# Two more row blocks' halves at the end: the last four tiles of a graph attention kernel as half tiles, in another order

## The reference

```python
XW = jnp.matmul(X, W)
s_col = jnp.matmul(XW, a[0, :f])
s_row = jnp.matmul(XW, a[0, f:])
Z1 = jax.nn.leaky_relu(s_row[:, None] + s_col[None, :], negative_slope=0.01)
den = jnp.exp(Z1)
num = jnp.matmul(A, den)
att = jnp.where(num != 0, den / jnp.where(num != 0, num, 1.0), 0.0)
H = jnp.matmul(A, jnp.matmul(att, XW))
x = _layernorm(x + H, axis=-1)
```

## Time and profile before

| | before |
|---|---|
| median of 3 runs | 309.93 us |
| the profiled execution's own time | 310.36 us |
| its span | 308.6 us |
| TensorE busy | 273.2 us (89%) |
| VectorE busy | 224.5 us (73%) |
| ScalarE busy | 190.1 us (62%) |
| GpSimd busy | 96.0 us (31%) |
| chain that ended last: TensorE's share | 62% |

### The profile page before, as it was taken

The page is one execution under the profiler, slowest core; times in us unless marked ns, Lnnn a source line. Parts: engine busy times, 40 slices in busy tenths (PEclk is TensorE's granted clock), DMA queues, the critical chain, the costliest instruction groups (busy, mean ns, idle before and its releaser), DMA issues.

```text
span 308.6 us, 5025 instructions
## 1 busy us (share of the span) xinstructions
PE 273.2 (89%) x1635; PEld 155.1 (50%) x1635; DVE 224.5 (73%) x363; ACT 190.1 (62%) x245; POOL 96.0 (31%) x95
## 2 busy tenths in 40 slices
PE   8793589788699999999999999999999726999994
PEld 3592337233244544544454445444444202999994
DVE  0778899999789989987985789898797710052275
ACT  2498068698899986959586788879688630000001
POOL 6501277998884644500000000066000063000000
PEclk9855556999999999999999999999999986999998
DMA  5000599707665343510000000001000053201111
GB/s 169 1 2 2 146 322 387 303 3 219 181 201 156 93 139 88 158 63 0 0 2 0 0 2 0 0 29 43 0 2 1 0 170 106 66 2 36 34 36 34
DMA packets 13940, 24.65 MB, mean 80 GB/s; under 512 B 1760, under 2 KB 8288, under 8 KB 13920
## 3 DMA queue, kind: packets, MB, share of 16 engines
q0 software_dynamic: 5632, 18.88, 19.1%
q1 hardware_dynamic: 8288, 5.50, 6.1%
HBM read 21.23 MB, written 3.15 MB: 79 GB/s over the span
## 4 chain that ended last, share of the span: by engine, by line
PE 62%; DVE 7%; ACT 6%; POOL 5%; issue 4%; DMA 4%; ACTq 1%; POOLq 0%; SPq 0%
PE ps L486 25%; PE ps L510 9%; PE ps L546 9%; PE ps L548 5%; PE ps L504 4%; POOL A L314 3%; PE ps L480 2%; PE ps L448 2%; PE ps L446 2%; PE ps L490 2%; DMA A<-adjT,perm 2%; POOL d_b L335 2%; ACT A L607 1%; ACT tmp L626 1%; DMA D<-d_b 1%
## 5 line engine op out<-in xcount | busy, mean ns | idle before, releaser
L486 PE MATMUL ps<-A,D 128*128 x372 | 86.3, 379 | 0.9 <-issue 0.2
L486 PEld LDWEIGHTS ps<-A,D 128*128 x372 | 36.2, 97 | 40.9 <-issue 10.1
L314 POOL DMA_INDIRECT A<-adjT,perm x31 | 45.5, 1468 | 28.3 <-DVE A L206 12.6
L335 POOL DMA_INDIRECT d_b<-crow,ranku x16 | 17.6, 1099 | 109.1 <-DVE crow L1014 71.0
L685 ACT ACTIVATE stage<-ps 128x1024 f32<-128x1024 f32 (+1 forms) x33 | 32.9, 997 | 25.8 <-PE ps L490 25.7
L996 DVE SCALAR_TENSOR_TENSOR stage<-ps,stage 128x1024 f32<-128x1024 f32 (+1 forms) x33 | 39.2, 1188 | 12.8 <-ACT stage L697 12.7
L546 PE MATMUL ps<-D,A 128*128 128x256 f16 x256 | 42.4, 273 | 1.0 <-DMA D<-d_b 1.0
L548 PE MATMUL ps<-D,A 128*128 128x128 f16 x256 | 42.3, 219 | 0.0
L1000 DVE SCALAR_TENSOR_TENSOR stage<-rrow,cfloor,stage 128x1024 f32<-128x1024 f32 (+1 forms) x33 | 41.3, 1252 | 1.3
L206 DVE SCALAR_TENSOR_TENSOR A<-A,ecol 128x1024 f16<-128x1024 f32 x31 | 38.8, 1277 | 1.0 <-ACT A L607 0.4
L687 ACT ACTIVATE stage<-stage,epst 128x1024 f32<-128x1024 f32 (+1 forms) x33 | 37.1, 1123 | 1.1
(11 more groups left out here) (187 smaller groups left out, 367.9 us busy)
## 6 DMA issues: line engine op xcount, KB each, us to landing
tmp<-xT SPq DMA_DIRECT2D x4, 256.0 KB, 4.1
d_xw<-stage SPq DMA_DIRECT2D x1, 1024.0 KB, 5.1
D<-d_b SPq DMA_DIRECT2D x4, 256.0 KB, 3.7
out<-crow SPq DMA_DIRECT2D x3, 256.0 KB, 2.3
A<-adjT,perm POOLq DMA_INDIRECT x31, 5.6
xws<-d_xw,perm POOLq DMA_INDIRECT x16, 3.6
d_b<-crow,ranku POOLq DMA_INDIRECT x16, 2.5
out<-crow SPq DMA_DIRECT2D x1, 128.0 KB, 1.8
```

The costliest lines, as they stand in the source:

```text
L314: nc.gpsimd.indirect_dma_start(out=raw[n], out_offset=None, in_=rows, in_offset=bass.IndirectOffsetOnAxis(ap=perm[:, 0, h, b:b + 1], axis= ...
L486: nc.tensor.matmul(num[bank + c], D[:, d, bass.ds(slot, 1), :], A[:, h, bass.ds(k, 1), a, c * W:(c + 1) * W], start=False, stop=False, ski ...
```

## The change

The last two row blocks of the second half, and no longer the last one alone, are half tiles. `ITEMS` lists all half tiles of the third quarter first and then those of the fourth, so the end of the list goes from (14 full), (15 third), (15 fourth) to (14 third), (15 third), (14 fourth), (15 fourth). `FULL` goes from 31 to 30 and `LAST` from 33 to 34. The second line keeps the set of items that use f16 parts as it is, 16 to 28.

```diff
-HALVED = NB - 1
+HALVED = NB - 2
 LAST = 2 * NB + NB - HALVED
 ITEMS = ([(t // NB, t % NB, 0, 2) for t in range(NB + HALVED)]
          + [(1, J, c, 1) for c in range(2) for J in range(HALVED, NB)])
@@
         def in_halves(t):
 
-            return NB <= t < FULL - 2
+            return NB <= t < FULL - 1
```

## The result

The changed kernel took 316.21 us, the median of 5 runs (315.27 to 316.83), against 310.09 us (309.92 to 310.81) before: 6.1 us slower, a ratio of 1.0183 with a 95% interval of 1.0162 to 1.0203. A second set of runs on another occasion gave 1.0177 (1.0142 to 1.0212). The time lies at the very edge of the predicted range (312.5 to 316.2), and next to the rival in which TensorE's clock falls in the new gap (315.9), not at the forecast of 313.4.

The account below looks back on a forecast made before the run. The prediction took the time as set by when the third quarter's transposes start (245.72 us) plus a fixed remainder. Bank wait, work behind it and end order move them to 249.15: 309.93 + 3.43 = 313.36, said as 313.4 us, range 312.5 to 316.2.

Parts of the forecast that it names:

- The fixed remainder behind the transposes: From the third quarter's transposes through GpSimd's scatters to the end: everything keeps its distance, nothing gives back the 3.43 us.
- First, the bank: Item 30 now takes bank 2, waits for item 29's read, starts at 236.68 not 232.62; TensorE idle 3.9 us.
- Second, the work from there: TensorE from item 30's start at 236.68: half tiles and L510s priced one by one, L510 of item 31 ending at 247.15.
- The second turn of the slot loop: In item 30's two-slot half tile: an estimated 0.10 us added for the branch, bounds 0 and 0.3.
- Third, the order at the end: Third quarter, complete at 247.2, waits behind item 32 on VectorE and TensorE; its transposes start at 249.15.
- The clock: TensorE's granted clock stays 1.00 from 232 to 250 us, through the new gap; this forecast had chance 0.73.
- The clock rival: TensorE's clock falls in the new gap: 2.5 us more, 315.9 us (317.6 with a later return); chance 0.21.
- The sum: Third quarter's transposes at 249.15 against 245.72, 3.43 us later, giving 313.4 us.

Follow-up runs that it names:

- e1: Changed kernel with 16 f16 matmuls that nothing reads put on TensorE ahead of item 30, filling the gap: 315.13 us, ratio 1.0165.
- e8: Second run of the changed kernel with the gap filled by 16 f16 matmuls that nothing reads: 315.43 us.
- e9: Changed kernel with the gap filled by four f32 matmuls in place of 16 f16 ones: 317.99 us in an uneven set, ratio 1.0125.
- e4: Changed kernel with its half tiles' banks swapped and the third quarter's end moved forward: 311.50 us, ratio 1.0031.
- e10: Changed kernel with banks swapped, third quarter's end moved forward, and two unread f32 matmuls between L510 of items 32 and 33: ratio 1.0005, uneven set.
- e5: Changed kernel with the gap filled by 16 unread matmuls and the third quarter's end moved forward: 315.48 us.
- e6: Kernel before, with item 30 (full tile) also waiting for item 29's read and 16 unread matmuls ahead of that wait: 314.59 us, ratio 1.0141.

## Why the prediction was right or wrong

- *The fixed remainder behind the transposes.* Right for the changed kernel: first scatter up 5.33, last 5.31, first L546 5.09. It is not a law, as e1 showed.
- *First, the bank.* Right to the row: 3.90 us of gap, released by item 29's L996; item 30 starts 8.62 us behind item 29, and not 4.46. Swapping the banks takes it away, and adding the wait to the old kernel brings it.
- *Second, the work from there.* 0.4 us too small, as the filled kernel shows at full clock. The second turn of the slot loop costs 0.36 us out of a wait (236.93 to 237.94 is 1.01, three matmuls are 0.65) and not 0.10; item 31 has a stop of 0.17 us behind its L480 (240.44) that I had not counted; item 32, which does not start from a wait, took 1.76 us and not 1.92; and the transposes start 0.96 and not 0.86 us behind L510. 0.26 + 0.19 - 0.16 + 0.10 = 0.39, and 3.43 + 0.39 is the 3.82 of e1 (3.81); e8 and e9 have 3.99 and 4.04.
- *Third, the order at the end.* Right in kind: about 2 us of the 4. To be faster, the prediction wanted the third quarter copied and transposed ahead of item 32, with the wait gone too. That has been tried (e4, e10), and is no gain so far: what is won at the first scatter is spent before the last one or behind it.
- *The clock.* This is the step that failed. I gave the 1.00 through the gap 0.73 and the fall 0.21. It fell in all four profiles. I had one empty stretch to go by, of 2.96 us, in the earlier trace rows, and took the dense work round the new gap for a reason against; a gap of 3.90, longer than one that had brought the fall, was the stronger evidence, and the Trainium skill's rule (TensorE: Matmul & The Clock Gate, "Why this matters for your kernels", against gaps between bursts of matmuls) said so too; here the trace agrees with it: the gap was 3.90 us, and the granted clock fell to 0.50.
- *The clock rival's size.* 2.5 us was too large for its own step: 0.7 to 1.5 us in the profiles, by the way it is measured. Counted from item 30's start, item 31 started 1.3 to 2.0 us later than in e1, not 2.5. In two of four profiles the low level lasted only 3.4 us. In the other two it lasted 6.8, and item 30 still cost 1.0 us more and not 1.5 (236.49 to 239.88, against 236.49 to 238.86 in e1): its six matmuls are one group of 2.74 us, without the stop of the second turn that e1 has. And 0.4 us of it came back behind: after the slow part item 31 ran L480 to L490 in 1.03 us and not 1.36, without the stops for issue.
- *The sum.* The profiled changed kernels are up 4.7 to 5.3 at the first scatter: 4.0 us for wait and order (e9), and 0.7 to 1.3 for the clock. The medians are up 6.1 and 5.3, and the first L546 in the profiles 4.75 to 5.09: 0.2 to 1.4 us are in no profile. That 316.2 lay so near to the rival's 315.9 is partly luck, its parts being 0.6 too small and 1.2 or more too large.

## What to carry to other kernels

When a loop's tail changes its tile size, work out for the first new tile which buffer it takes and who read it last; a rotation that is free of stalls for one parity can wait for its immediate predecessor for the other. An idle stretch of TensorE can be priced twice, once as the wait and once in the matmuls behind it, and one idle stretch in the trace that brought the clock down is to be taken at its word. Filling a gap with matmuls that nothing reads tells the two prices apart, but look at what the added instructions move, and finish an experiment in its profile, not at its time.

## What the runs showed of the hardware

- TensorE's clock fell 2.05 us after its last matmul in the changed kernel (232.59 to 234.64) and 2.96 us after it in the kernel before, 1.30 us after it in e4, and in two profiles 0.8 and 1.4 us after work had begun again. So the place of the fall does not depend on the gap alone.
- Where an instruction packet (0.02 MB, by its rhythm TensorE's) fell on the last scatter, in e1, e8 and e5, that scatter landed after 2.9 to 3.4 us; in the profiles without one it took 2.2. In these three kernels 16 matmuls stand ahead of item 30, and the packet comes at 261 us and not at 268; with four f32 matmuls (e9), or with the 16 in the kernel before with the wait (e6), it stays behind the scatters.
- The matmuls meant to bring the clock up ahead of the last product held it up by about 1 us in one profile (e10), where the clock stayed low through nearly all 14 of them (5.95 us, against 4.48 before).
